# Two-layer transformer block on one core: the left-over expert slots with the tokens as the stationary operand, in four column groups, and their products for four sequences at once

## The reference

```python
capacity = max(1, int(Sz * CAP_FACTOR / E) + 1)          # 512 * 2 / 8 + 1 = 129
scores = softmax(einsum('bsd,ed->bse', x, router_w))      # E = 8 experts
gate_vals, sel_idx = top_k(swapaxes(scores, 1, 2), capacity)
tokens = x[b_idx, sel_idx]                                # 129 tokens for each sequence and expert
h = gelu(einsum('becd,edh->bech', tokens, w1) + b1)       # hidden 512
y = einsum('bech,ehd->becd', h, w2) + b2
out = zeros_like(x).at[b_idx, sel_idx].add(y * gate_vals[..., None])
```

## Time and profile before

| | us |
|---|---|
| median of 3 runs | 760.32 |
| lowest, highest | 759.8, 760.71 |
| the profiled execution, its own time | 760.39 |
| its span, first to last instruction | 758.6 |
| TensorE busy in the span | 624.1 |
| VectorE busy | 528.8 |
| GpSimd busy | 372.1 |
| ScalarE busy | 370.3 |

### The profile page before, as it was taken

One profiled execution on the slowest core, in us unless ns is written; L12 is line 12 of the kernel. 1 busy time (PEld: TensorE's weight loads), 2 busy tenths in 40 slices (PEclk: granted clock), 3 DMA queues, 4 the chain that ended last, 5 costly groups with the idle time before them and its releaser, 6 DMA issues.

```text
span 758.6 us, 14495 instructions
## 1 busy us (share of the span) xinstructions
PE 624.1 (82%) x4251; PEld 386.8 (51%) x4287; DVE 528.8 (70%) x1785; ACT 370.3 (49%) x794; POOL 372.1 (49%) x507
## 2 busy tenths in 40 slices
PE   2379998997602999999889768999999999998894
PEld 1246666555401588776666533445454545443553
DVE  8468888888786013224578859898989898987554
ACT  0332233320270423325632357777777777767773
POOL 0075565554102787776887554343434343443341
PEclk9999999999956899999999989999999999999998
DMA  9400000000050232235663333030204020400021
GB/s 298 129 0 1 1 1 0 0 1 1 1 152 14 53 41 42 39 66 111 100 106 33 31 76 58 4 65 5 62 9 61 9 60 11 57 5 2 17 57 41
DMA packets 45145, 34.56 MB, mean 46 GB/s; under 512 B 4304, under 2 KB 41728, under 8 KB 45072
## 3 DMA queue, kind: packets, MB, share of 16 engines
q1 hardware_dynamic: 33584, 25.15, 14.1%
q0 software_dynamic: 10144, 7.90, 7.7%
q10 hardware_dynamic: 1344, 0.62, 0.3%
HBM read 14.13 MB, written 9.70 MB: 31 GB/s over the span
## 4 chain that ended last, share of the span: by engine, by line
PE 62%; DVE 19%; issue 8%; ACT 4%; DMA 2%; SPq 1%; POOL 1%; DVEq 0%; ACTq 0%; POOLq 0%
PE bank L2074 8%; PE bank L1211 8%; PE wide L1203 7%; DVE masked L1672 6%; PE wide L2061 5%; PE bank L2010 4%; PE wide L652 4%; PE wide L653 3%; PE bank L624 3%; DVE prod L402 2%; PE wide L634 2%; PE bank L2086 1%; DVE st L305 1%; DVE mx L1672 1%; PE wide L2010 1%
## 5 line engine op out<-in xcount | busy, mean ns | idle before, releaser
L1869 ACT ACTIVATE pexp<-wide 128x512 f32<-128x512 f32 (+2 forms) x384 | 180.9, 535 | 78.4 <-PE wide L2061 75.3
L1800 POOL TENSOR_SCALAR_AFFINE_SELECT pexp<-pexp 128x256 f32<-128x256 f32 x256 | 107.1, 432 | 167.5 <-ACT pexp L1869 166.0
L1672 DVE CUSTOM_DVE_ANT_0 masked<-bank,mask_qk 128x384 f32<-128x384 f32 (+3 forms) x376 | 164.2, 482 | 35.1 <-PE bank L2010 32.8
L2061 PE MATMUL wide<-qT,kTe 128*128 128x256 bf16 (+3 forms) x501 | 119.3, 299 | 7.7 <-ACT pexp L1869 2.8
L964 POOL DMA_INDIRECT x_dram<-yg,row_u x56 | 89.3, 1595 | 30.2 <-DVE yg L1016 15.3
L2010 PE MATMUL bank<-kTm,qT 128*128 128x128 bf16 (+3 forms) x365 | 85.8, 298 | 17.0 <-DVE mx L1672 13.1
L1153 ACT ACTIVATE hT<-wide,b1T 128x512 f32<-128x512 f32 x64 | 43.9, 686 | 101.4 <-PE wide L1203 101.4
L2074 PE MATMUL bank<-pexp,vx 128*32 128x512 f32 (+3 forms) x1024 | 86.2, 449 | 4.9 <-POOL pexp L1800 4.9
L973 POOL DMA_INDIRECT x_row<-xln_dram,row_u x64 | 63.0, 985 | 52.6 <-DVE slot_tok L843 33.6
L1672 DVE CUSTOM_DVE_ANT_0 masked<-wide,mask_qk 128x512 f32<-128x512 f32 (+3 forms) x136 | 64.7, 499 | 14.8 <-PE wide L2010 14.8
L578 POOL TENSOR_TENSOR kv<-kx,qv 128x1024 f32<-128x1024 f32 x32 | 62.4, 1951 | 23.8 <-PE wide L653 23.7
(11 more groups left out here) (280 smaller groups left out, 1024.7 us busy)
## 6 DMA issues: line engine op xcount, KB each, us to landing
qT<-qp SPq DMA_DIRECT2D x126, 64.0 KB
x_sb<-in_L_attn_x SPq DMA_DIRECT2D x8, 256.0 KB, 6.6
w_sb<-in_L_ffn_w SPq DMA_DIRECT2D x1, 2048.0 KB, 12.9
xln_dram<-hT SPq DMA_DIRECT2D x8, 256.0 KB, 2.3
x_dram<-x_sb SPq DMA_DIRECT2D x7, 256.0 KB, 2.7
x_sb<-x_dram SPq DMA_DIRECT2D x7, 256.0 KB, 3.0
out_x<-x_sb SPq DMA_DIRECT2D x7, 256.0 KB, 2.3
qT<-qp_first SPq DMA_DIRECT2D x18, 64.0 KB
```

Source lines behind the costliest of these rows:

```text
L1672: ins = nc.vector.tensor_tensor_reduce(out=masked[:, n % 4, at], in0=bank_of(n)[:, at], in1=mask_qk[:, T - w:T], scale=1.0, scalar=LEAST, ...
L1800: nc.gpsimd.affine_select(out=pexp[:, at, :, 0:P], in_=pexp[:, at, :, 0:P], pattern=[[0, 2], [1, P]], compare_op=ALU.is_ge, fill=0.0, base ...
L1869: nc.scalar.activation(pexp[:, exp_slot(b, 2 * step + h // 2), h % 2:h % 2 + nh, 0:w], scores_bank(b, m)[:, 0:nh * w].rearrange("p (h t) - ...
L2061: ins = nc.tensor.matmul(scores_bank(b, m)[:, hh * w:(hh + 1) * w], kTe[:, par, j * P:(j + 1) * P], qT[:, b % QB, 4 * qd + h + hh, j * P:T ...
```

## The change

The last slots are turned round. In phase 1 the transposed tokens are copied to `xlT` [128, 8 experts, 32], of which 8 columns an expert are filled and the rest is zero. In phase 2 the tokens of an expert are the stationary operand (32 columns), and w1 of that expert, 512 columns, is streamed: four experts in the four column groups of one bank, eight matmuls into two banks (bank 0 and bank 6). VectorE copies both banks out. In phase 3, a new fill, eight transposes bring the hidden rows back, and VectorE adds b1. In phase 4 the hidden columns (8) are the stationary operand and w2 (128 columns) is streamed, again in four column groups, 32 matmuls. VectorE adds b2 in four pieces. SyncE then moves the rows into the order of the slots with eight small transfers, and VectorE waits for these in phase 5 before it spreads them. The shares of all sequences are formed in phase 6: in step (6, k), for token tile k, two matmuls of 32 rows and 512 columns, one for sequences 0 to 3 into bank 0 and one for 4 to 7 into bank 6. ScalarE keeps the first, VectorE adds the second to x. Fill k waits until fill k - 1 was taken by both. The share of sequence 0 is added by VectorE in phase 7. SyncE writes x of sequences 4 to 7 to DRAM after all four fills. The diff, cut to its core:

```diff
-        xlT = scratch("xlT", [P, BE])
+        xlT = scratch("xlT", [P, E, 32])
-        ylT = scratch("ylT", [P, B, E])
+        h_last, yl_rows, y_last = masked[:, 0:2, :], masked[:, 2, 0:2 * D], masked[0:BE, 3, 0:D]
-        side = bank[0]
+        side = (bank[0], bank[6])
-        LAST_AT = {1: LAST_XT, 2: LAST_HIDDEN, 4: LAST_OUTPUT, 5: LAST_T}
+        LAST_AT = {1: LAST_XT, 2: LAST_HIDDEN, 3: LAST_HT, 4: LAST_OUTPUT, 5: LAST_ROWS}
+        REST_P, LAST_FILLS = 6, 4
@@ moe_sync
+            sp.wait_ge(m_taken, LAST_FILLS)
+            for g in range(G):
+                for j in range(E // G):
+                    sp.dma_start(y_last[j * G + g:BE:E, :], yl_rows[32 * g:32 * g + B, j * D:(j + 1) * D]).then_inc(m_yr, 16)
+            sp.wait_ge(m_taken, LAST_FILLS + NT)
             for b in DMA_SECOND:
-                sp.wait_ge(m_taken, fill_no["rest", b])
                 x_to_dram(sp, b, 1)
@@ dve_moe_last
             if stage_no == LAST_XT:
+                dve.wait_ge(m_xz, 1)
+                nc.vector.tensor_copy(xlT[:, :, 0:B], side[0][:, 0:BE].rearrange("p (b e) -> p e b", e=E)).then_inc(m_taken, 1)
             elif stage_no == LAST_HIDDEN:
+                nc.vector.tensor_copy(h_last[:, 0, :], side[0][:, :])
+                nc.vector.tensor_copy(h_last[:, 1, :], side[1][:, :]).then_inc(m_taken, 1)
+            elif stage_no == LAST_HT:
+                for j in range(E // G):
+                    ins = nc.vector.tensor_tensor(hl_in[:, j * G:(j + 1) * G, :, :]..., side[j]..., b1T..., ALU.add)
             elif stage_no == LAST_OUTPUT:
+                for g in range(G):
+                    rows = slice(32 * g, 32 * g + B)
+                    ins = nc.vector.tensor_tensor(yl_rows[rows, :]..., side[0][rows, 0:E // G * D]..., b2rep[rows, g::G, :], ALU.add)
             else:
+                dve.wait_ge(m_yr, 16 * E)
+                nc.vector.tensor_tensor(rest_r[0:BE, :, :], y_last.unsqueeze(1).broadcast_to([BE, B, D]),
+                                        by_seq, ALU.mult).then_inc(m_rr, 1)
+        def dve_moe_fold_rest(dve, k):
+            dve.wait_ge(m_full, LAST_FILLS + k + 1)
+            nc.vector.tensor_tensor(x_sb[:, G:B, k, :], x_sb[:, G:B, k, :], side[1]..., ALU.add).then_inc(m_taken, 1)
+        def act_moe_keep_rest(act, k):
+            act.wait_ge(m_full, LAST_FILLS + k + 1)
+            nc.scalar.activation(masked[:, k, :], side[0][:, :], ACT.Copy).then_inc(m_kept, 1)
+        def dve_moe_first_rest(dve):
+            dve.wait_ge(m_kept, NT)
+            nc.vector.tensor_tensor(x_sb[:, 0], x_sb[:, 0], masked[:, :, 0:D], ALU.add).then_inc(m_first, 1)
@@ moe_dve, for p in range(E)
                 for b in BY_PE:
                     dve_moe_place(dve, p, b)
                 if p in LAST_AT:
                     dve_moe_last(dve, LAST_AT[p])
+                if p == REST_P:
+                    for k in range(NT):
+                        dve_moe_fold_rest(dve, k)
+                if p == REST_P + 1:
+                    dve_moe_first_rest(dve)
                 dve_moe_gated(dve, p)
@@ TensorE
+        def pe_moe_rest(pe, k):
+            pe.wait_ge(m_rr, 1)
+            pe.wait_ge(m_taken, LAST_FILLS + k)
+            pe.wait_ge(m_kept, k)
+            for half in range(2):
+                rows = slice(32 * half, 32 * half + 32)
+                ins = nc.tensor.matmul(side[half][:, :], rest_l[rows, k * P:(k + 1) * P],
+                                       rest_r[rows, G * half:G * half + G, :]..., start=True, stop=True)
+            ins.then_inc(m_full, 1)
+        def pe_moe_last(pe, stage_no, j):            # in steps (p, 1) and (p, 2), as j = 0 and 1
+            pe.wait_ge(m_taken, stage_no)
             elif stage_no == LAST_HIDDEN:
+                for g in range(G):
+                    ins = nc.tensor.matmul(side[j][32 * g:32 * g + 32, :], xlT[:, j * G + g, :], w1_sb[:, j * G + g, :], ...)
+            elif stage_no == LAST_HT:
+                for c in range(HC):
+                    ins = nc.tensor.transpose(side[j][:, c * P:(c + 1) * P], h_last[:, j, c * P:(c + 1) * P], ident)
+            else:
+                pe.wait_ge(m_lh, 1)
+                for c in range(HC):
+                    for g in range(G):
+                        e = j * G + g
+                        ins = nc.tensor.matmul(side[0][32 * g:32 * g + B, j * D:(j + 1) * D], hl[:, e, c, :], w2_sb[:, e, c, :], ...)
```

More of the change, by code:

```diff
@@ L1103, in moe_dve @@
                     dve_mqa_buffers(dve)
-                if (p, 0) in REST_AT and REST_AT[p, 0] in DMA_SECOND:
-                    dve_moe_fold_rest(dve, REST_AT[p, 0])
+                if p == 0:
+                    nc.vector.memset(xlT[:, :, :], 0.0).then_inc(m_xz, 1)
                 for b in BY_PE:
@@ L1224, in pe_moe_scatter @@
             ins.then_inc(m_placed, 1)
-        def pe_moe_rest(b, into, start, stop):
-            for k in range(NT):
-                ins = nc.tensor.matmul(into[:, k * D:(k + 1) * D], rest_l[:, k * P:(k + 1) * P],
-                                       rest_r[:, b, :], start=start, stop=stop)
-            return ins
-        def pe_moe_last(pe, stage_no, i):
-            if fill_no["last", stage_no] > 1:
-                pe.wait_ge(m_taken, fill_no["last", stage_no] - 1)
-            two = range(E // G * i, E // G * (i + 1))
-            ins = None
-            if stage_no == LAST_XT and i == G - 1:
+        def pe_moe_rest(pe, k):
+            pe.wait_ge(r_last.sem, r_last.total(1))
+            pe.wait_ge(m_rr, 1)
[4 more added lines that the diff above has]
+                ins = nc.tensor.matmul(side[half][:, :], rest_l[rows, k * P:(k + 1) * P],
+                                       rest_r[rows, G * half:G * half + G, :].rearrange("r b d -> r (b d)"),
+                                       start=True, stop=True)
+            ins.then_inc(m_full, 1)
@@ L1255, in pe_moe_last @@
-            if i == G - 1:
+            if j:
                 ins.then_inc(m_full, 1)
```

104 lines of the change are left out of this document (42 added, 62 removed).

## The result

| | us |
|---|---|
| before, median of the 4 runs beside it | 760.06 (758.65 to 760.71) |
| changed kernel, median of 4 runs | 753.91 (753.5 to 754.78) |
| ratio, with its 95% interval | 0.993 (0.9914 to 0.9946) |
| its span | 752.2 (before 758.6) |
| busy in the span: TensorE, VectorE, GpSimd, ScalarE | 616.6, 532.1, 371.1, 370.8 |

The account below looks back on a forecast made before the run. TensorE fills the chain, but GpSimd's 10.9 us a phase bounds the gain: 6.1 (GpSimd's waits) + 1.9 (VectorE's slack) - 0.3 (port loss) - 1.6 (clock) = 6.1, so 754.3 us from 760.39; range 750.5 to 758.5.

Parts of the forecast that it names:

- TensorE's gain, 10.5 to 13.5: Phases 1 to 7: 24.8 us of TensorE work removed, 11.3 to 14.3 added, leaving a gain of 10.5 to 13.5 us.
- the 4 to 7 us: Phase 6: four pairs of share matmuls, 4 us in all if the row tiles overlap, 7 if not.
- The stall in (6, 1): Step (6, 1): fill 1 waits until VectorE has added fill 0, behind its place, costing TensorE 1.4 us.
- GpSimd's 6.1: First half: GpSimd's real waits for outputs, 6.1 us, are all it can gain; the last scatters start that much earlier.
- the 0.3 that VectorE beside it was to cost: GpSimd beside VectorE's new copies and additions: one longer transfer, 0.3 us lost, between 0 and 1.
- VectorE's 1.9 of slack: Behind the read-back of x: VectorE began its additions 1.9 us after the landing, so it gains that much more.
- The clock's 1.6: Step (9, 3): TensorE idles 2.5 to 5.5 us, then runs at half speed, losing 1.6 us, between 0 and 2.
- The edits costed at nothing: Eight small transfers from phase 4, earlier writes of x and ScalarE's fourth kept tile: all taken as hidden, no cost.
- A: Rival: TensorE's whole gain goes through, giving 747 to 750 us; chance 7%.
- B: Rival: TensorE waits for gathers and the clock falls each time, or landings slow; 757 to 759 us; chance 15%.
- C: Rival: the clock stays low in phases 6 to 8, making the kernel slower, some 772 us; chance 5%.
- D: Rival: an unseen wait holds the read-back where it was, so no change, 760 us; chance 5%.

Follow-up runs that it names:

- run 2: The changed kernel with all work of the last slots left out (zeros added in their place): 752.79 us, ratio 0.9914.
- run 8: The changed kernel without GpSimd's eight scatters of sequence 1, so a GpSimd phase is 9.0 us: 748.53 us, ratio 0.986.
- run 7: The kernel before without GpSimd's eight scatters of sequence 1, so a GpSimd phase is 9.0 us: 761.15 us, ratio 1.0013.
- run 9: The changed kernel with VectorE making sequence 0's query parts behind the first of its three additions, not the third: 753.06 us, ratio 0.9901.
- run 10: The early query parts of run 9 put into the kernel of run 5: 755.55 us, ratio 0.9944.
- run 11: The changed kernel with GpSimd's scatters of phase 7 ahead of its gathers for phase 11: 755.28 us, ratio 0.9937.
- run 5: The changed kernel with the last slots turned round but the shares formed as before, in phases 6 and 7: 752.03 us, ratio 0.9912.
- run 4: The changed kernel with four unused filler matmuls in TensorE's idle time before sequence 0's key and value product: 750.6 us, ratio 0.9869.
- run 12: The kernel of run 9 with three unused filler matmuls ahead of the transposes of step (10, 0): 751.25 us, ratio 0.9898.
- run 3: The changed kernel with each pair of share products in phase 6 formed twice: 753.24 us over 7 runs, interval 0.9886 to 0.9948.

## Why the prediction was right, step by step

**TensorE's gain, 10.5 to 13.5: 12.6.** The new blocks take what the column groups of the earlier trace rows said, or less. In phase 2 a set of four column groups takes 1.0 us, as taken; in phase 4 16 matmuls of 128 columns take 0.99 us, 0.25 a set of four and not the 0.35 that the attention's gave, so 2.0 us for the eight sets and not 2.8. The two row tiles, which no row of before showed, start together:

```profile
297.32 1.06 PE L1279 MATMUL bank<-w_sb,hl 128*8 128x128 f32 x32
298.31 1.16 PE L1231 MATMUL bank<-w_sb,hT 128*128 128x128 f32 x8
...
313.73 0.69 PE L1254 MATMUL bank<-rest_r,rest_l 32*128 32x512 f32 x1
313.73 0.69 PE L1254 MATMUL wide<-rest_r,rest_l 32*128 32x512 f32 x1
314.26 0.59 PE L1254 MATMUL bank<-rest_r,rest_l 32*128 32x512 f32 x1
314.27 0.59 PE L1254 MATMUL wide<-rest_r,rest_l 32*128 32x512 f32 x1
314.78 1.16 PE L1231 MATMUL bank<-w_sb,hT 128*128 128x128 f32 x8
```

1.05 us a pair (314.78 - 313.73), the near end of the 4 to 7 us. The Trainium skill's figure that the prediction named (TensorE: Matmul & The Clock Gate, "Measured speedup vs the span model"), for four row tiles, points the same way; the pair shows the overlap for two. The sum took what was removed as differences of steps, but what was added as the blocks' own lengths, and these aren't the same: the output behind a block takes 1.16 us instead of 1.05. As steps, the sets of phase 2 and those of phase 4 cost 2.3 us each and phase 6 6.4 with its stall, so that 12.4 were added, still within the 11.3 to 14.3. A pair costs 1.26 us as a step (below, 3.01 less a bare 1.75), as much as the four matmuls of one sequence did before (1.28): the new shares gain because there are four of them and not eight.

```profile
323.13 1.16 PE L1231 MATMUL bank<-w_sb,hT 128*128 128x128 f32 x8
...
326.14 1.16 PE L1231 MATMUL bank<-w_sb,hT 128*128 128x128 f32 x8
```

The stall in (6, 1) is there with 1.37 us, predicted 1.4:

```profile
319.07 0.66 PE L1254 MATMUL bank<-rest_r,rest_l 32*128 32x512 f32 x1 [1.37 <-DVE x_sb L1070]
```

**GpSimd's 6.1: 5.7,** and the 0.3 that VectorE beside it was to cost is about the difference, though not at the place named. Without any last slots (run 2) it is 6.6, so what they cost GpSimd is rather 0.9. The two copies out of PSUM, which the prediction named, cost nothing: a scatter that began inside one took 1.56 us. Five of GpSimd's 54 instructions are longer than their like, and each began while VectorE worked on operands in SBUF: a gather of 1.14 us inside the spreading of the rows (309.25, shown below), which now reads `y_last` from SBUF (before it read PSUM, and the gather inside it took 0.98), a scatter of 1.89 and a gather of 1.29 inside multiplications by the gate (313.26, 328.06), gathers of 1.11 and 1.06 inside a cast and the setting of the 0/1 matrix. Of these only the spreading is new work; the others stand in the kernel before too, and meet other transfers now. In run 8 the gather began 0.08 us behind the start of the same spreading, and took twice its time:

```profile
308.28 2.03 POOL L976 DMA_INDIRECT x_row<-xln_dram,row_u  x1 [0.30 <-issue]
```

Runs 2, 7 and 8 show the bound itself. The Trainium skill has the name of this state (Perfetto Trace Analysis, "What "DMA-bound" means"): the sequencer track of the issuing engine is solid with DMA instructions. The trace agrees: 54 of them with 0.30 us between.

**VectorE's 1.9 of slack: 1.9.** 7.7 at the third addition less 5.8 at the read-back. VectorE's wait of 5.05 us for the landing is the sign that was named for it.

**The clock's 1.6:** the idle time was forecast at 2.5 to 5.5 us and was 4.41, and the clock fell behind it, as said. The gain at the gated outputs of phase 9 is 6.4 us (366.63 - 266.30 less 361.83 - 267.94), 1.8 less than the 8.3 at the product ahead of it. But it didn't last to the end, as the sum has it: at the last instruction the gain is 8.0 again. One piece of it can be named: the first max product comes 7.6 us earlier. Before, TensorE stood idle for 0.88 us ahead of it while SyncE still sent the query rows; now it doesn't (that these rows were the cause is inferred). So in the profiled executions the expert stage and what follows gained 8.0, and 1.6 of that went in the later first scatter; by the medians the gain is 6.2 to 6.7. That the total fell so near to the forecast is luck in part: the 1.6 us of the clock's term isn't in the profiled end, and 1.6 us that the forecast didn't have stands ahead of the stage. Whether the medians' missing 1.3 to 1.8 us are the clock behind the key and value product or the part before the first scatter stays open: both profiles of the changed kernel point to the latter (they start 1.6 and 1.1 us later than the one of before), but one profile of before is too little to decide it.

**The edits costed at nothing** cost nothing, one of them with a thinner cover than was written. The eight small transfers took 5.03 us to issue, and the prediction had them needed 9 to 10 us after their start. VectorE was ready for them after 5.7:

```profile
303.14 5.03 SPq L957 DMA_DIRECT2D masked<-masked  x8
...
309.25 1.22 DVE L1064 TENSOR_TENSOR rest_r<-masked,cst 64x1024 f32<-64x1024 f32 x1 [0.42 <-DMA masked<-masked]
```

The 0.42 us lie ahead of gated outputs that GpSimd didn't need yet.

**The rivals.** A (TensorE's whole gain, 747 to 750) fell for the reason given against it, and run 8 shows that it holds once GpSimd's period is 9.0. B, C and D didn't come. B's mechanism exists in a small form: TensorE waited 0.90 us for gathers at step (9, 0), and the clock stayed up. In run 9 it waited 2.94 us and the clock fell, and in run 2, with nothing left of the last slots, it is there in full: five such waits, and a fall behind two of them.

## What to carry to other kernels

A gain on the engine that fills the chain goes through only until the engine with the next longest period has no wait left. So add up that engine's instructions by phase, and its waits for the first engine: here 7.3 us of waits with 1.2 us of its own gaps in them, and 1.9 us of slack behind the read-back, said what 12.6 us would be worth in that half. After the change the same sum says what to do next: in this kernel 12 us less of TensorE in the first half were worth under 1 us (run 2), and 15 us less of GpSimd 5 us (run 8), until TensorE was the bound again. A smaller step of GpSimd wasn't tried.

Compare two traces from an event where the part that differs begins, not from zero. And move a step past a wait only after looking at what the engine meets next: three such moves (runs 9, 10, 11) gave no measurable gain or a loss, since each exchanged one wait for another.

## What wasn't expected of the hardware

- Matmuls with 8 columns as stationary operand, in four column groups, took 0.25 us for four of 128 float32 columns, where the attention's with 32 columns take 0.35. Whether the width or the work between them makes the difference wasn't tried.
- GpSimd's gathers and scatters were longer when they began well inside a multiplication, an addition or a cast of VectorE whose operands all lie in SBUF: a gather took up to 2.03 us instead of about 0.98 (run 8). Inside instructions that read PSUM, copies and additions alike, and inside the statistics of x they kept their 0.94 to 1.02 and 1.55 to 1.62 us. This is read from some eighty overlaps in six traces; no run was made for it.
- Filling an idle time of TensorE with useless matmuls made the kernel faster, 3 us in the median, of which the profiled pair shows 1 behind the first scatter. A fall of the clock costs some 1.6 to 1.8 us where it is seen in a trace.
- The length of the last idle time alone doesn't tell whether the clock falls. It fell behind 2.94, 4.41, 4.93 and 7.34 us (runs 9, the changed kernel, 10, 11) and stayed up behind 0.74 and 1.34 (runs 5 and 4). But in run 12, with fillers ahead, it stayed up behind 2.64, and in run 3 it fell to 0.55 in the stretch from 358 to 360 us, with only 1.91 of idle time ahead of the product at 356.18. In run 2 it stayed up behind 2.25 us at 301.15 and fell behind 2.25 us at 333.46.
- Runs of one kernel spread more in some of these kernels than in the others: 753.21 to 754.24 for the changed one, 750.16 to 754.73 with the early parts, 749.55 to 760.16 with the shares twice. Within a kernel the longer executions have the lower mean granted clock (run 3: 0.961 in its fastest, 0.944 in its slowest). Why some kernels spread more isn't known.
